# Last inverses of the channel part interleaved with the next part, flipped rows loaded in halves, constants loaded later, and some results stored later, in a four-layer spectral-convolution kernel

## The reference, cut to what matters

```python
# layers 0, 2, 3
xs = rfft2(x, axes=(1, 2)).reshape(B, H, W // 2 + 1, 8, 48)
o1 = relu(xs @ w1 + b1)            # complex, by block
o2 = softshrink(o1 @ w2 + b2, 0.01)
x  = irfft2(o2) + x
# layer 1
X_k  = fftn(x).real + fftn(x).imag         # over batch, h, w and channels
X_nk = roll(flip(x, (1, 2)), (1, 1), (1, 2))
s    = mix(X_k, X_nk)                      # two block products, relu between them
x    = dht(softshrink(s, 0.01)) / size + x
```

## Time and profile before

| | |
|---|---|
| median of 3 runs | 1066.89 us (1064.87 to 1070.45) |
| the profiled execution | 1066.92 us, its span 1065.0 us |
| PE busy | 934.6 us, 88% of the span |
| DVE, ACT, POOL busy | 575.1, 476.4, 80.6 us |
| mean granted clock of PE | 0.943 of 2.4 GHz |
| DMA | 184.37 MB, mean 173 GB/s |

### The profile page before, as it was taken

The page is one execution under the profiler, slowest core; times in us unless marked ns, Lnnn a source line. Parts: engine busy times, 40 slices in busy tenths (PEclk is TensorE's granted clock), DMA queues, the critical chain, the costliest instruction groups (busy, mean ns, idle before and its releaser), DMA issues.

```text
span 1065.0 us, 14258 instructions
## 1 busy us (share of the span) xinstructions
PE 934.6 (88%) x5168; PEld 472.4 (44%) x5168; DVE 575.1 (54%) x869; ACT 476.4 (45%) x757; POOL 80.6 (8%) x156
## 2 busy tenths in 40 slices
PE   2789997999899987799999968999999999999803
PEld 1445554755666655244444423444443344344401
DVE  2156453444345856387775455666666666666401
ACT  1345443444345423243334414665565555556501
POOL 3011111111011100000001020000000000000000
PEclk7899998999899998799999988999999999999956
DMA  9888497469548785853345314444654575451572
GB/s 308 282 253 285 126 310 283 116 174 302 174 142 264 227 277 178 204 139 100 94 116 112 102 51 122 110 117 116 198 160 119 163 226 162 141 200 48 121 187 118
DMA packets 94110, 184.37 MB, mean 173 GB/s; under 512 B 12439, under 2 KB 72113, under 8 KB 92250
## 3 DMA queue, kind: packets, MB, share of 16 engines
q1 hardware_dynamic: 84218, 142.33, 46.3%
q0 software_dynamic: 9824, 41.14, 11.6%
HBM read 104.29 MB, written 79.14 MB: 172 GB/s over the span
## 4 chain that ended last, share of the span: by engine, by line
PE 75%; DMA 12%; DVE 5%; issue 3%; ACT 2%; SPq 1%; POOL 0%; ACTq 0%; DVEq 0%; POOLq 0%
PE psum L877 16%; PE psum L886 15%; PE psum L916 8%; PE psum L969 6%; PE psum L993 6%; PE psum L953 6%; PE psum L865 5%; PE psum L896 4%; DMA RG<-rows_along_h 4%; DMA RX<-rows_along_w 3%; PE psum L927 3%; PE psum L980 3%; DMA rows_along_w<-RX 2%; PE psum L942 1%; PE psum L842 1%
## 5 line engine op out<-in xcount | busy, mean ns | idle before, releaser
L1290 DVE SCALAR_TENSOR_TENSOR RA<-psum,RA 112x896 f32<-112x896 f32 (+1 forms) x120 | 124.3, 1036 | 240.1 <-ACT RA L1145 240.1
L1145 ACT ACTIVATE RA<-psum,small 112x896 f32<-112x896 f32 (+1 forms) x120 | 115.8, 965 | 97.9 <-PE psum L886 97.3
L886 PE MATMUL psum<-RA,RW 112*64 112x448 f32 (+1 forms) x640 | 133.6, 539 | 2.7 <-ACT RA L1136 2.7
L1136 ACT ACTIVATE RA<-psum,RW 112x448 f32<-112x448 f32 (+1 forms) x160 | 89.3, 610 | 87.6 <-PE psum L877 87.6
L916 PE MATMUL psum<-RD,const 128*128 128x384 f32 (+1 forms) x304 | 99.5, 448 | 10.2 <-DVE RA L1250 5.5
L1250 DVE COPY RD<-psum 128x672 f32<-128x672 f32 (+2 forms) x120 | 68.5, 572 | 65.3 <-PE psum L916 62.2
L865 PE MATMUL psum<-const,RX 128*112 128x128 f32 x528 | 69.4, 284 | 22.7 <-DMA RX<-rows_along_w 22.7
L1130 ACT ACTIVATE RA<-psum 128x384 f32<-128x384 f32 (+2 forms) x72 | 50.6, 703 | 84.3 <-PE psum L865 50.3
L1275 DVE TENSOR_TENSOR RX<-RX,RA 112x768 f32<-112x768 f32 (+2 forms) x80 | 80.7, 1009 | 1.5
L1130 ACT ACTIVATE RD<-psum 128x384 f32<-128x384 f32 (+2 forms) x120 | 63.1, 526 | 39.0 <-PE psum L916 37.5
L865 PEld LDWEIGHTS psum<-const,RX 128*112 128x112 f32 x528 | 62.0, 182 | 41.5 <-issue 37.9
(11 more groups left out here) (100 smaller groups left out, 1097.8 us busy)
## 6 DMA issues: line engine op xcount, KB each, us to landing
RG<-rows_along_h SPq DMA_DIRECT2D x7, 3072.0 KB, 11.0
rows_along_h<-RD SPq DMA_DIRECT2D x96, 144.0 KB, 3.5
rows_along_w<-RX SPq DMA_DIRECT2D x56, 224.0 KB, 5.6
RX<-x SPq DMA_DIRECT2D x16, 768.0 KB, 8.0
out<-RA POOLq DMA_DIRECT2D x16, 768.0 KB, 4.3
rows_along_h<-RD SPq DMA_DIRECT2D x64, 168.0 KB, 2.8
RX<-rows_along_w SPq DMA_DIRECT2D x12, 672.0 KB, 7.2
spectrum<-RA POOLq DMA_DIRECT2D x48, 168.0 KB, 5.4
```

Source lines behind the costliest of these rows:

```text
L886: mm = nc.tensor.matmul(bank[b * HALF:(b + 1) * HALF, a * BANK:a * BANK + nk * H], w4[layer][0:ROWS, g, b, a], hidden(slot)[0:ROWS, b * N: ...
L1136: done = nc.scalar.activation(hidden(slot)[0:ROWS, b * N:b * N + nk * H], banks(key)[0:ROWS, b, 0:nk * H], ACT.Relu, bias=bias[layer][0:RO ...
L1145: nc.scalar.activation(dst, src, ACT.Relu, bias=minus_lambda_l0 if key[0] == "S4" else minus_lambda).then_inc(act_emptied, 1)
L1290: nc.vector.scalar_tensor_tensor(out=dst, in0=src, scalar=LAMBDA / 64 if key[0] == "S4" else LAMBDA, in1=dst, op0=ALU.add, op1=ALU.min).th ...
```

## The change

1. **Order.** 6A of passes 0 and 1 starts a round later (20 instead of 19); 6C of pass 2 starts in round 38 instead of 41. In the channel part CF(2, 1) comes before H1(1, 2), and CI(7, 0) before H2(9, 0). CI of items 8 and 9 move into rounds 1, 2 and 3 of part C.
2. **Start.** Part 3 of pass 0 gets a stage area of its own in RD. Constants are loaded in two pieces after the stage stores, the first weights after the first row group, the inverse constants after group 2. x of pass 2 is loaded 4 rounds later.
3. **Flipped rows.** Those of odd items are kept in two halves in other places; each half is loaded when it can be. The low half for item 1 needs only pass 2's flipped rows.
4. **DVE.** The sums of y(2) move to H2(0, 0), those of y(3) and the joining of item 2 are spread over the last flip, join(0) and join(1) move to CI(6, 1) and CI(7, 0).
5. **Waits.** TC and 5C wait for the stored results later; step 3's update is loaded after H1(9, 1); POOL holds quarters 2 and 3 of pass 2's results until the last part of G is loaded.

```diff
@@ -82,11 +82,11 @@
 def flip_round(p):
-    return 10 * p + (18 if p == PASSES - 2 else 19)
+    return 10 * p + (18 if p == PASSES - 2 else 20)
...
 def last_inverse_round(p):
-    return 10 * p + (16 if p < PASSES - 2 else 21)
+    return 10 * p + (16 if p < PASSES - 2 else 18)
@@ -122,32 +122,38 @@
     o += [("6A", PASSES - 1, g, v) for g in range(PASS_PAIRS) for v in range(FLIP_UNITS)]
-    for z in range(1, ITEMS + 2):
-        if z < ITEMS:
-            o += [("H1", z, 0), ("H1", z, 1)]
-        if z < ITEMS:
-            if 2 <= z + 1 < ITEMS:
-                o += [("CF", z + 1, 0)]
-            o += [("H2", z, 0)]
-        if z >= 2:
+    for z in range(1, ITEMS):
+        o += [("H1", z, 0), ("H1", z, 1)]
+        if z + 1 < ITEMS:
+            o += [("CF", z + 1, 0)]
+        if z == ITEMS - 1:
             o += [("CI", z - 2, 0)]
-        if z < ITEMS:
-            o += [("H1", z, 2), ("H1", z, 3)]
-            if 2 <= z + 1 < ITEMS:
-                o += [("CF", z + 1, 1)]
+        o += [("H2", z, 0)]
+        if z == 1:
+            o += [("CF", 2, 1)]
+        elif z < ITEMS - 1:
+            o += [("CI", z - 2, 0)]
+        o += [("H1", z, 2), ("H1", z, 3)]
+        if 1 < z < ITEMS - 1:
+            o += [("CF", z + 1, 1)]
...
             o += [("CI", z - 2, 1)]
-        if z < ITEMS:
-            o += [("H2", z, 1)]
+        o += [("H2", z, 1)]
...
             o += [("3L2", r)]
+        if r == 1:
+            o += [("CI", ITEMS - 2, 0)]
+        elif r in (2, 3):
+            o += [("CI", ITEMS - 1, r - 2)]
...
             o += [("4L2", r)]
+        if r == 1:
+            o += [("CI", ITEMS - 2, 1)]
@@ -312,6 +318,8 @@
         def stage(p, k):
+            if (p, k) == (0, X_PARTS - 1):
+                return RD[:, D_SLOTS * TURN_COLS:D_SLOTS * TURN_COLS + STAGE_COLS]
@@ -393,8 +401,11 @@
         assert 8 * N + V3 + V4 + INV <= G_COLS
-        an1, s_sum0, s_sum1 = in_region(RG, G_COLS, [PAIRS * N] * 3)
-        assert 3 * PAIRS * N <= G_COLS
+        s_sum0, s_sum1 = in_region(RG, G_COLS, [PAIRS * N] * 2)
+        assert 2 * PAIRS * N <= G_COLS
+        an1_low, = in_region(RX, Y_SLOTS * 4 * STEP_COLS, [PASS_PAIRS * N])
+        an1_high, = in_region(RA, 3 * PAIRS * N, [PASS_PAIRS * N])
+        assert Y_SLOTS * 4 * STEP_COLS + PASS_PAIRS * N <= b_at and 3 * PAIRS * N + PASS_PAIRS * N <= A_SLOTS * STEP_COLS
@@ -416,7 +427,8 @@
         result = [a.rearrange("p (t s n) -> p t s n", t=2, s=2) for a in (r0, r1)]
-        an = [by_pair(a) for a in (an0, an1)]
+        an = [[by_pair(a) for a in halves]
+              for halves in ((an0[:, 0:PASS_PAIRS * N], an0[:, PASS_PAIRS * N:]), (an1_low, an1_high))]
@@ -446,6 +458,7 @@
         consts_loaded = sem("consts_loaded")
+        inverse_loaded = sem("inverse_loaded")
@@ -558,6 +571,7 @@
             first, n_first = const_at["dft_w"]
+            at_inv = const_at["inv_h"][0]
@@ -615,11 +629,6 @@
                 load_x(0, k)
-            sp.dma_start(const[:, n_first:], consts[:, n_first:]).then_inc(consts_loaded, 16)
-            sp.dma_start(RW[:, 0:W3], conv_w3[0]).then_inc(conv_loaded[0], 16)
-            sp.dma_start(RW[0:ROWS, W3:W3 + W4], conv_w4[0]).then_inc(conv_loaded[0], 16)
-            sp.dma_start(RW[0:ROWS, W3 + W4:], conv_bias[0]).then_inc(conv_loaded[0], 16)
-            sp.dma_start(l1_bias_sb, l1_bias).then_inc(conv_loaded[0], 16)
@@ -645,15 +654,14 @@
-            def load_an(z):
+            def load_an(z, half):
...
                 src = flipped[b].rearrange("(g s c) n -> s c g n", s=2, c=BS)
-                for half in range(2):
-                    g = slice(half * PASS_PAIRS, (half + 1) * PASS_PAIRS)
-                    for s in range(2):
-                        sp.dma_start(an[b][s * HALF:s * HALF + BS, g, 0:n], src[s, :, g, n0:n0 + n]
-                                     ).then_inc(an_loaded[b][half], 16)
+                g = slice(half * PASS_PAIRS, (half + 1) * PASS_PAIRS)
+                for s in range(2):
+                    sp.dma_start(an[b][half][s * HALF:s * HALF + BS, :, 0:n], src[s, :, g, n0:n0 + n]
+                                 ).then_inc(an_loaded[b][half], 16)
@@ -663,8 +671,15 @@
                 store_stage(0, k, 2)
-            for e in range(BM_SLOTS):
+            sp.dma_start(const[:, n_first:at_inv], consts[:, n_first:at_inv]).then_inc(consts_loaded, 16)
+            load_bm(0)
+            sp.dma_start(RW[:, 0:W3], conv_w3[0]).then_inc(conv_loaded[0], 16)
+            sp.dma_start(RW[0:ROWS, W3:W3 + W4], conv_w4[0]).then_inc(conv_loaded[0], 16)
+            sp.dma_start(RW[0:ROWS, W3 + W4:], conv_bias[0]).then_inc(conv_loaded[0], 16)
+            sp.dma_start(l1_bias_sb, l1_bias).then_inc(conv_loaded[0], 16)
+            for e in range(1, BM_SLOTS):
                 load_bm(e)
+            sp.dma_start(const[:, at_inv:], consts[:, at_inv:]).then_inc(inverse_loaded, 16)
@@ -682,8 +697,9 @@
                         store_stage(p, k, 4)
-                        if p + 1 < PASSES:
-                            load_x(p + 1, k)
+                    k -= 4 if p == 1 else 0
+                    if 0 <= k < X_PARTS and p + 1 < PASSES:
+                        load_x(p + 1, k)
@@ -704,19 +720,24 @@
                         wait_flipped_stored(sp, 1, g)
-                    load_an(0)
+                    for half in range(2):
+                        load_an(0, half)
...
             load_y(3)
+            for g in range(PASS_PAIRS):
+                wait_flipped_stored(sp, PASSES - 2, g)
+            load_an(1, 0)
...
                 wait_flipped_stored(sp, PASSES - 1, g)
-            load_an(1)
+            load_an(1, 1)
...
             for z in range(ITEMS - 2):
-                wait_filled(sp, ("H1", z, PAIRS - 1))
-                load_an(z + 2)
+                for half in range(2):
+                    wait_filled(sp, ("H1", z, PASS_PAIRS * (half + 1) - 1))
+                    load_an(z + 2, half)
@@ -731,6 +752,8 @@
                     wait_updated_c(sp, "J", s - R_SLOTS)
+                if s == R_SLOTS - 1:
+                    wait_filled(sp, ("H1", ITEMS - 1, PASS_PAIRS - 1))
@@ -766,9 +789,8 @@
-            for m in range(STAGE_SLOTS):
-                at = STAGE_AT + m * STAGE_COLS
-                pad = RX[:, at:at + STAGE_COLS].rearrange("p (m r) -> p m r", r=ROWS)[:, :, BS:HALF]
+            for k in range(X_PARTS):
+                pad = stage(0, k).rearrange("p (m r) -> p m r", r=ROWS)[:, :, BS:HALF]
@@ -817,6 +839,8 @@
                     wait_emptied(pool, ("6C", p, 2 * k + 1))
+                    if (p, k) == (PASSES - 2, X_PARTS // 2):
+                        pool.wait_ge(g_loaded[(PASSES - 1) % 2], g_uses(2 * PASSES - 1))
@@ -963,11 +987,11 @@
                 bank = take(key)
-                for s, src in enumerate((kf[b], an[b])):
+                for s, src in enumerate((kf[b][:, g], an[b][g // PASS_PAIRS][:, g % PASS_PAIRS])):
...
                         mm = nc.tensor.matmul(bank[0:ROWS, r * BANK:r * BANK + n], v3_view[rows, s, g],
-                                              src[rows, g, 0:n], start=s == 0, stop=s == 1)
+                                              src[rows, 0:n], start=s == 0, stop=s == 1)
@@ -1018,6 +1042,8 @@
                 elif stage == "5A":
+                    if key == ("5A", 0, 0):
+                        pe.wait_ge(inverse_loaded, 16)
@@ -1099,12 +1125,15 @@
             if p == 0 and v == 0:
-                eng.wait_ge(pads_zeroed, STAGE_SLOTS)
+                eng.wait_ge(pads_zeroed, X_PARTS)
             m = p * X_PARTS + v // 2 - STAGE_SLOTS
-            if v % 2 == 0 and m >= 0:
+            if v % 2 == 0 and p > 0:
...
         def wait_turn_free(eng, e):
+            if e == ALL_GROUPS:
+                for b in range(B):
+                    eng.wait_ge(result_stored[b], 48 * PASS_GROUPS)
@@ -1232,9 +1261,8 @@
                     e = s // PASS_PAIRS
-                    if s == 0:
-                        for b in range(B):
-                            act.wait_ge(result_stored[b], 48 * PASS_GROUPS)
+                    if s == PASS_PAIRS:
+                        act.wait_ge(result_stored[0], 48 * PASS_GROUPS)
@@ -1457,13 +1485,11 @@
                     copy(*s6a_views(key, 1)).then_inc(vec_emptied, 1)
-                    if key == ("6A", PASSES - 1, 0, 1):
-                        sum_sides(2)
-                        sum_planes(2)
-                    elif key == ("6A", PASSES - 1, 1, 1):
+                    if key == ("6A", PASSES - 1, 0, 2):
                         sum_sides(3)
+                    elif key == ("6A", PASSES - 1, 1, 0):
                         sum_planes(3)
-                    elif key == ("6A", PASSES - 1, 1, 3):
+                    elif key == ("6A", PASSES - 1, 1, 2):
@@ -1497,6 +1523,9 @@
                             sign(2)
+                    if z == 0 and h == 0:
+                        sum_sides(2)
+                        sum_planes(2)
@@ -1519,15 +1548,16 @@
```

(9 more changed lines are left out.)

## The result

The changed kernel takes **1034.07 us** (median of 4 runs, 1031.69 to 1035.83), the kernel before on the same chip 1068.67 (4 runs, 1064.87 to 1070.55): a ratio of **0.9679**, 95% interval 0.9641 to 0.9717. The forecast was 1026 with a range from 1010 to 1044. The profiled execution has a span of 1033.4 us where it was 1065.0, so the trace has 31.6 us to account for.

What follows compares the result with a forecast made beforehand. TensorE, busy 934.6 of 1065.0 us, is the floor; only its idle and half-speed time can go. Terms -4 - 15 + 1 - 16 - 6.5 = -40.5 against 1066.9 give 1026 us, range 1010 to 1044 (own range 1017 to 1036).

Steps and rivals of the forecast that it cites:

- First flips: 6A of passes 0 and 1, a round later: both waits for rows along h and the half speed go, -15 us.
- Last inverses: Inverses of items 8 and 9 mixed into part C's first rounds: waits and half speed there go, -16 us.
- The -17.5 worked out: Last inverses: end of round 2 plus the last inverse reached at 640.3 instead of 657.8 us.
- Last flip: Pass 3's flip, rows in halves: wait of 9.55 us goes, but y(4) is late next; net +1 us.
- 12.7 us of idling: Last flip: PE idles this long before H1(2,0), held by VectorE and y(4), then runs at half speed, costing about 3.
- Rival (a): VectorE isn't held by y(4) and the start is free of group 3: 1010 us, chance 0.12.
- Start: Kernel start: PE begins S2 8.6 us earlier, but its wait for group 3 grows from 2.1 to 5.6; -4 us.
- At the 382 GB/s of the saturated stretch that is 17.8 us: Start: time to move 6.8 MB of x and stage stores, from 1.2 us on, putting PE's start at 24.7.
- The second step: Start: load of row group 3 lands at 64.9 us, where PE would stand ready at 59.3.
- rival (b): The loads stay last: both flip loads slip with the round and the start gives nothing; 1044 us, chance 0.17.
- Tail: Kernel end, pass 2's results three rounds earlier, half held: last rows along h land sooner, net -6.5 us.
- -8 with +1.6, +1 and +0.3: Tail: landing gain -7 to -9; costs of three moved units, an earlier result sharing engines in round 41, held results.

Runs made afterwards that it cites:

- a_y4: Changed kernel with the load of y(4) issued right behind that of y(3): 1020.5 us, ratio 0.9534 to the kernel before.
- a_r21: Changed kernel with pass 2's inverse starting in round 41 again and POOL holding nothing back: 1035.7 us, ratio 0.9692 to the kernel before.
- a_nohold: Changed kernel without POOL's wait, so quarters 2 and 3 of pass 2's results go out when ready: 1036.3 us, ratio 0.9688.

## Why the prediction was right, and where it was off

The total fell inside the range because two large terms, flips and inverses, held. The errors of start and tail go the same way and add up to 9.6 us; the flips, 2.4 us better than forecast, took some of that back.

- **First flips: right**, in mechanism and size (-15 forecast, -17.4 in the trace, -18.0 alone). Reading a round's length against the landing was enough. The margin, put at 0.8 us, was 0.3, so that it sufficed is in part luck.
- **Last inverses: right** (-16, -15.4, -17.6 alone). The -17.5 worked out is what the boundary itself gave (about -17); the 2 us lost at 705.56 belong to a place that the prediction didn't look at.
- **Last flip: right** (+1, +0.9), and for the reason given: y(4) is late next. The forecast of 12.7 us of idling stands against 13.83. One reading was wrong: VectorE didn't wait long for y(4) before, the bracket of the earlier trace rows is 0.29 us. Rival (a) was excluded by this wait, and a_y4 shows its price: 13.6 where I had put 12.
- **Start: wrong by 5.5 us.** The step that failed is "At the 382 GB/s of the saturated stretch that is 17.8 us": stage stores by themselves go at 276 to 293, the last of them landed at 25.13, and the first S2 came at 29.78 instead of 24.7. The second step, that the load of group 3 goes ahead with PE's lead and lands at 64.9, failed too: it landed at 70.36, where it had been 69.89. SP's issue of it had moved from 39.77 to 35.68, but the matrix ahead of it was issued at 34.19, where it had been 34.75; when the matrix was through, no row shows. The mechanism named there, one transfer in a single piece, is right; I had not drawn from it that it also fixes the landing, so that any lead gained before it turns into wait. Here rival (b)'s "the start gives nothing" was right.
- **Tail: mis-sized by 4.1 us.** The gain on the landing was right (-7 to -9; -7.2 against the kernel before, -7.8 against a_r21). The sum was not: -8 with +1.6, +1 and +0.3 makes -5.1, and -6.1 at best, not -6.5. Of the costs, the three units were sized well (1.6 forecast, 1.9 measured), the slower clock at the last product had no term (1.3), and the 0.3 for held results is right by a_nohold (8.60 against 8.44 us to the last issue). The rest is no step of the prediction: the wait of 1.10 us at 840.72, and the end behind the last issue, 17.0 us where it was 14.6, whose spread has no cause that was found.
- The 1.3 us lost in the rest of part A had no term. They are the half speed behind a wait of 2.7 us that every kernel here has, and that only some pay for.

## What to carry to other kernels

When two loads bind the same place, making one early shows nothing; look at the issue time of the second, and whether its queue stood idle before (here 30 us). A lead gained ahead of a transfer that ends at a fixed time becomes a wait of the same length: cut that transfer first. Before you charge a moved unit with a delay, compare the two traces at the point just ahead of it: of 5.3 us that looked like the price of the tail, 2.15 were there before.

## What was not expected of the hardware

- The stage stores, almost alone, keep the DMA engines 0.93 to 1.04 busy and move 276 to 293 GB/s, the mixed traffic from 30 to 45 us moves 391 at 1.03. Busy share isn't rate.
- The single-piece load of the forward matrix cost 0 to 2 us with the start of before and 6.7 with that of the change, at the same place in the queue.
- The last load, of 12 partitions in each of its four transfers, runs at 90 and then 57 GB/s with nothing beside it (granted clock 0.50, PE idle); cut in quarters it is complete 14.7 us after its first issue instead of 15.5, but its first quarter is there 5.0 us after it, and the cut is worth about 8 us.
- The same wait of 2.7 us at the end of part A is followed by four records of 1.53 us in all or of 2.90, in executions of nearly the same work.
